# The first batch's input products of a selective scan on GpSimd instead of VectorE, with three state buffers

## The reference, cut to what matters

```python
def step(state, inp):
    d, b, c, u = inp
    dA = jnp.exp(d[..., None] * A)
    state = state * dA + (d * u)[..., None] * b[:, None, :]
    y = jnp.einsum('bdn,bn->bd', state, c)
    return (state, y)
```

## Time and profile before

| what | us |
|---|---|
| median of 3 runs | 1496.59 (1494.74 to 1496.68) |
| the profiled execution | 1496.58 |
| its span in the trace | 1494.8 |
| TensorE busy | 1345.9 (90% of the span) |
| VectorE busy | 1028.1 (69%) |
| ScalarE busy | 695.4 (47%) |
| GpSimd busy | 89.2 (6%) |

### The profile page before, as it was taken

How to read it: one execution, slowest core, us unless ns; L and a number is a source line. 1 busy time by engine, 2 the same in 40 slices (tenths; PEclk the granted TensorE clock), 3 DMA queues, 4 the chain that set the end, 5 groups by cost and what they waited for, 6 DMA issues and landing times.

```text
span 1494.8 us, 16001 instructions
## 1 busy us (share of the span) xinstructions
PE 1345.9 (90%) x5768; PEld 661.1 (44%) x5768; DVE 1028.1 (69%) x1219; ACT 695.4 (47%) x1477; POOL 89.2 (6%) x116
## 2 busy tenths in 40 slices
PE   5757668999999799899999799899999899799999
PEld 2324444444444365444444365444444355444443
DVE  5699996689979645789897844779897944521110
ACT  5345653465542285375552277365562187121110
POOL 0000001000000000000000000100000000100000
PEclk8955669999999799999999889999999999799999
DMA  6286661157765700137765610117775530012102
GB/s 232 46 197 145 136 146 29 53 138 189 189 148 126 176 2 1 43 106 181 180 162 141 164 45 2 39 53 189 190 166 144 144 83 2 0 33 63 59 25 85
DMA packets 53277, 158.80 MB, mean 106 GB/s; under 512 B 5072, under 2 KB 10704, under 8 KB 44752
## 3 DMA queue, kind: packets, MB, share of 16 engines
q0 software_dynamic: 9216, 67.11, 22.6%
q1 hardware_dynamic: 25664, 54.23, 11.1%
q10 hardware_dynamic: 18320, 36.45, 8.1%
HBM read 86.20 MB, written 4.46 MB: 61 GB/s over the span
## 4 chain that ended last, share of the span: by engine, by line
PE 68%; DVE 20%; ACT 6%; DMA 3%; issue 3%; ACTq 0%; POOL 0%; DVEq 0%
PE ps_a L854 21%; PE ps_a L866 10%; DVE state L1048 7%; PE ps_a L934 6%; PE ps_b L874 5%; PE ps_a L780 4%; PE ps_w L833 4%; PE ps_w L742 4%; PE ps_b L794 3%; DMA y_sb<-state 3%; DVE state L1053 3%; DVE state L1043 3%; ACT r L583 2%; DVE neg_max L1083 2%; PE ps_w L900 2%
## 5 line engine op out<-in xcount | busy, mean ns | idle before, releaser
L854 PE MATMUL ps_a<-xt,w_sb 128*128 128x512 f32 x704 | 319.2, 607 | 0.0
L1048 DVE TENSOR_TENSOR_SCAN state<-decay,state 128x2048 f32<-128x2048 f32 x64 | 282.7, 4418 | 2.1 <-DVE state L1043 0.5
L854 PEld LDWEIGHTS ps_a<-xt,w_sb 128*128 128x128 f32 x704 | 137.2, 196 | 173.2 <-issue 172.8
L635 ACT ACTIVATE r<-ps_a 128x512 f32<-128x512 f32 x132 | 78.8, 597 | 257.5 <-PE ps_a L866 137.5
L583 ACT ACTIVATE r<-ps_a,neg_max 128x128 f32<-128x128 f32 (+3 forms) x256 | 134.6, 542 | 131.8 <-DVE neg_max L1083 126.0
L1219 DVE TENSOR_TENSOR r<-r,ps_a 128x512 f32<-128x512 f32 x132 | 90.2, 685 | 149.9 <-ACT r L635 149.9
L934 PE MATMUL ps_a<-wd_sb,r 128*128 128x512 f32 x352 | 164.1, 617 | 17.0 <-DMA wd_sb<-in_w_down 16.8
L541 ACT ACTIVATE decay<-dt_sb,decay_rate 128x511 f32<-128x511 f32 x256 | 163.4, 711 | 30.1 <-DVE state L1048 29.7
L866 PE MATMUL ps_a<-r,wb_sb 128*128 128x512 f32 x352 | 166.6, 596 | 2.2 <-DVE r L1219 2.2
L780 PE MATMUL ps_a<-r 32*128 32x512 f32 (+3 forms) x512 | 125.7, 572 | 44.1 <-ACT r L583 40.0
L1043 DVE TENSOR_TENSOR state<-du_sb,bc_sb 128x2048 f32<-128x2048 f32 x64 | 146.2, 2284 | 7.8 <-DMA y_sb<-state 5.7
(11 more groups left out here) (117 smaller groups left out, 1385.3 us busy)
## 6 DMA issues: line engine op xcount, KB each, us to landing
y_sb<-state POOLq DMA_DIRECT2D x64, 1024.0 KB, 9.3
bc_sb<-bc_rows ACTq DMA_DIRECT2D x64, 512.0 KB, 6.1
w_sb<-in_w_tiles SPq DMA_DIRECT2D x44, 512.0 KB, 8.7
wd_sb<-in_w_down SPq DMA_DIRECT2D x44, 256.0 KB, 3.2
wb_sb<-in_w_adapt SPq DMA_DIRECT2D x44, 128.0 KB, 2.1
xa<-in_x SPq DMA_DIRECT2D x4, 1024.0 KB, 5.2
out_x<-xb SPq DMA_DIRECT2D x16, 256.0 KB, 8.0
xn_att<-in_ctx_t SPq DMA_DIRECT2D x4, 512.0 KB, 7.9
```

What stands on the lines that cost most here:

```text
L854: mm = nc.tensor.matmul(ps_a[:, 2 * (f % 2) + half, :], w_sb[:, slot, at + k * P:at + (k + 1) * P], xt[:, k, :], start=(k == 0), stop=Fals ...
L1048: nc.vector.tensor_tensor_scan(flat, decay[:, n % 2, :, :].rearrange("p j l -> p (j l)"), flat, 0.0, ALU.mult, ALU.add).then_inc(scan_chai ...
```

## The change

For batch 0 alone, the pieces `mul` of the states 1 to 15 leave VectorE; GpSimd does them as `spread` (state 0 stays on VectorE). GpSimd issues the add of `n` and then does `spread(n + 2)` (`spread(1)` comes first, as soon as `du_sb` is there). The state tiles and the row pairs of batch 0 go round three buffers instead of two: the third state tile lies in `r2`, the third pair of rows in the first half of `w_sb`'s first buffer. Therefore `spread(n)` waits for the add of `n - 3`, the load of row pair `n` for `out` of `n - 3`, and the first two loads of `w_sb` wait for the last `out` of batch 0. The table for batch 0 has 34 pieces instead of 49, again one in each of the eleven parts of the projections and the rest spread over 31 steps. The other batches keep their pieces, and only count their semaphores differently.

```diff
+FIRST_RING = 3
-def plan(counts):
+def plan(counts, first=False):
     pieces = [("du", 0)]
     for n in range(NS):
-        pieces += [("mul", n), ("run", n), ("out", n)]
+        pieces += [("mul", n)] * (n == 0 or not first) + [("run", n), ("out", n)]
...
-        slots[at["du", 0] if n < 2 else between(at["out", n - 2], at["mul", n])]["bc"].append(n)
+        ring = FIRST_RING if first else 2
+        used = at["mul", n] if ("mul", n) in at else at["run", n]
+        slots[at["du", 0] if n < ring else between(at["out", n - ring], used)]["bc"].append(n)
...
+PIECES_FIRST = 2 + 2 * NS
-PLAN_FIRST = plan([0] * DOWN + [1] * FT + spread_over(PIECES - FT, STEPS - LAST_STEPS) + [0] * LAST_STEPS)
+PLAN_FIRST = plan([0] * DOWN + [1] * FT + spread_over(PIECES_FIRST - FT, STEPS - LAST_STEPS) + [0] * LAST_STEPS, True)
...
+        states_first = [state[:, 0, :, :], state[:, 1, :, :], r2[:, 4:8, :]]
+        rows_first = [bc_sb[:, 0, :, :], bc_sb[:, 1, :, :], w_sb[:, 0, :].rearrange("p (c l) -> p c l", c=2)]
...
             def load_w(t, f):
                 if f >= 2:
                     sp.wait_ge(gu_ready, t * EVALS + EVAL_AT[f - 2, 0] + 1)
+                elif t == 0:
+                    sp.wait_ge(scan_chain, chain(0, NS - 1, 3))
                 else:
                     sp.wait_ge(scores_ready, t * STEPS + 1)
...
+            def spread(n):
+                if n == 1:
+                    pool.wait_ge(du_ready, 1)
+                if n >= FIRST_RING:
+                    pool.wait_ge(y_added, 16 * (n - FIRST_RING + 1))
+                slot, count = bc_use(0, n)
+                pool.wait_ge(bc_loaded[slot], 16 * count + 16)
+                row = rows_of(0, n)[:, 0, :].unsqueeze(1).to_broadcast([P, JT, L])
+                nc.gpsimd.tensor_tensor(state_of(0, n), du_sb[:], row, ALU.mult).then_inc(spread_ready, 1)
+
             def add_states(b, slot):
                 for n in slot["add"]:
...
+                    if b == 0 and n + 2 < NS:
+                        spread(n + 2)
...
             inverse_deviation("att", 0)
+            spread(1)
...
                 elif kind == "run":
...
-                    dve.wait_ge(scan_chain, base + 1)
+                    if b == 0 and n > 0:
+                        dve.wait_ge(spread_ready, n)
+                    else:
+                        dve.wait_ge(scan_chain, chain(b, n, 1))
```

More of the change, by code:

```diff
@@ L105, with chain, bc_use @@
 LAST_STEPS = 1
-PLAN_FIRST = plan([0] * DOWN + [1] * FT + spread_over(PIECES - FT, STEPS - LAST_STEPS) + [0] * LAST_STEPS)
+PLAN_FIRST = plan([0] * DOWN + [1] * FT + spread_over(PIECES_FIRST - FT, STEPS - LAST_STEPS) + [0] * LAST_STEPS, True)
 PLAN_NEXT = plan(IN_EVALS + spread_over(IN_DOWN, FT - FREE_DOWN) + [0] * FREE_DOWN +
                  spread_over(PIECES - sum(IN_EVALS) - IN_DOWN, STEPS - LAST_STEPS) + [0] * LAST_STEPS)
+def chain(b, n, k):
+    return 2 * n + k if b == 0 else PIECES_FIRST - 1 + (b - 1) * 3 * NS + 3 * n + k
+def bc_use(b, n):
+    if b == 0:
+        return n % FIRST_RING, n // FIRST_RING
+    slot = n % 2
+    return slot, (NS - slot + FIRST_RING - 1) // FIRST_RING + (b - 1) * (NS // 2) + n // 2
 def projections(f):
@@ L236, in decoder_layer, with state_of, rows_of @@
         xdt_sb = sb("xdt_sb", [P, L])
+        states_first = [state[:, 0, :, :], state[:, 1, :, :], r2[:, 4:8, :]]
+        rows_first = [bc_sb[:, 0, :, :], bc_sb[:, 1, :, :], w_sb[:, 0, :].rearrange("p (c l) -> p c l", c=2)]
+        def state_of(b, n):
+            return states_first[n % FIRST_RING] if b == 0 else state[:, n % 2, :, :]
+        def rows_of(b, n):
+            return rows_first[n % FIRST_RING] if b == 0 else bc_sb[:, n % 2, :, :]
         u_sb, xin_sb, conv_sb = state[:, 0, :, :], decay[:, 0, :, :], decay[:, 1, :, :]
@@ L305, in decoder_layer @@
         dt_ready = sem("dt_ready")
-        bc_loaded = [sem(f"bc_loaded{k}") for k in range(2)]
+        bc_loaded = [sem(f"bc_loaded{k}") for k in range(FIRST_RING)]
+        spread_ready = sem("spread_ready")
         decay_ready = sem("decay_ready")
@@ L461, in add_states @@
                     pool.dma_start(y_sb[:].rearrange("p j l -> p (j l)"),
-                                   state[:, n % 2, :, :].rearrange("p j l -> p (j l)"),
+                                   state_of(b, n).rearrange("p j l -> p (j l)"),
                                    accum_op=ALU.add).then_inc(y_added, 16)
+                    if b == 0 and n + 2 < NS:
+                        spread(n + 2)
             def attention(b, slots):
@@ L509, in split_first @@
                 if not first_batch(b):
-                    for k in range(2):
-                        act.wait_ge(bc_loaded[k], 16 * (NS // 2) * b)
+                    for n in range(NS - (FIRST_RING if b == 1 else 2), NS):
+                        slot, count = bc_use(b - 1, n)
+                        act.wait_ge(bc_loaded[slot], 16 * count + 16)
                 act.wait_ge(xdt_ready, b + 1)
@@ L523, in load_bc @@
                         act.wait_ge(bc_stored, 16 * b + 16)
[L524 to L527, removed]
+                    ring = FIRST_RING if b == 0 else 2
+                    if n >= ring:
+                        act.wait_ge(scan_chain, chain(b, n - ring, 3))
+                    elif b > 0:
+                        act.wait_ge(scan_chain, chain(b - 1, NS - 1, 3))
                     pair = bc_rows.rearrange("(c n) l -> n c l", c=2)[n]
-                    act.dma_start(bc_sb[:, n % 2, :, :], pair.unsqueeze(0).to_broadcast([P, 2, L]))\
-                        .then_inc(bc_loaded[n % 2], 16)
+                    act.dma_start(rows_of(b, n), pair.unsqueeze(0).to_broadcast([P, 2, L]))\
+                        .then_inc(bc_loaded[bc_use(b, n)[0]], 16)
             def make_decay(b, slot):
@@ L1032, in scan_piece @@
                     return
-                base = b * 3 * NS + 3 * n
-                flat = state[:, n % 2, :, :].rearrange("p j l -> p (j l)")
+                flat = state_of(b, n).rearrange("p j l -> p (j l)")
                 if kind == "mul":
@@ L1040, in scan_piece @@
                         dve.wait_ge(y_added, 16 * (b * NS + n - 1))
-                    dve.wait_ge(bc_loaded[n % 2], 16 * (NS // 2) * b + 16 * (n // 2) + 16)
-                    row = bc_sb[:, n % 2, 0, :].unsqueeze(1).to_broadcast([P, JT, L])
-                    tt(state[:, n % 2, :, :], du_sb[:], row, ALU.mult).then_inc(scan_chain, 1)
+                    slot, count = bc_use(b, n)
+                    dve.wait_ge(bc_loaded[slot], 16 * count + 16)
+                    row = rows_of(b, n)[:, 0, :].unsqueeze(1).to_broadcast([P, JT, L])
+                    tt(state_of(b, n), du_sb[:], row, ALU.mult).then_inc(scan_chain, 1)
                 elif kind == "run":
@@ L1050, in scan_piece @@
                 else:
-                    dve.wait_ge(scan_chain, base + 2)
-                    row = bc_sb[:, n % 2, 1, :].unsqueeze(1).to_broadcast([P, JT, L])
-                    tt(state[:, n % 2, :, :], state[:, n % 2, :, :], row, ALU.mult).then_inc(scan_chain, 1)
+                    dve.wait_ge(scan_chain, chain(b, n, 2))
+                    row = rows_of(b, n)[:, 1, :].unsqueeze(1).to_broadcast([P, JT, L])
+                    tt(state_of(b, n), state_of(b, n), row, ALU.mult).then_inc(scan_chain, 1)
             def rotate(b, f):
```

4 lines of the change are left out of this document (2 added, 2 removed).

## The result

The changed kernel takes 1529.79 us (median of four, 1526.06 to 1534.03) against 1496.61 (1494.74 to 1496.68): 1.0226 times as long, with an interval of 1.0193 to 1.0258. The direction was predicted and the size was not: 1509 was forecast, with 1525 as the upper end. The profiled execution took 1526.06 us with a span of 1524.1, 29.3 longer than before; in the other three the granted clock of TensorE was 0.902, 0.897 and 0.896 instead of 0.903, and the time longer with it. What follows explains the profiled 29.3; the 3.7 us by which the median lies above this execution were not traced.

What follows compares the result with a forecast made beforehand. VectorE was taken to bound batch 0's attention (busy 140.0 of 142 us), with adds close beneath at 10.1 us a state. +3.1 us in front and +9.3 in the attention gave +12.4, from 1496.58 to 1509 us; range 1482 to 1525.

Steps and rivals of the forecast that it cites:

- turns over SBUF for a whole instruction: `run` or `out` and `spread` exclude each other for whole instructions, first come first served; 1509 us, chance 0.75.
- the stretch in front: Ahead of batch 0's attention: `spread(1)` hidden, later products delay VectorE, `out(4)` ends at 109.5 instead of 106.44, +3.1 us.
- the edits at no cost: Late `w_sb` loads, covered by 39.8 us, row pairs loaded a state ahead and the last add's landing cost nothing.
- who goes first: In attention gaps of one step `run` precedes `spread`, 11.91 us a state, seven states; with two steps `spread` precedes, 13.17, three.
- second kind: Attention state with two steps ahead of `run`, so `spread` goes first: 1.26 + 4.42 + 4.32 + 0.98 + 2.19 = 13.17 us.
- the worst case of the turns: All ten attention states have `spread` first: 140.2 us, +18.1 and +3.1, total 1518.
- the terms of a state: Attention prices: `spread` 4.42 us, asking 1.26 behind `out`; step 0.98, `run` 4.32, `out` 2.19.
- The state behind them: Attention state after the ten, with no `spread` and two steps: 8.5 us.
- No exclusion: Rival: `spread` runs beside VectorE, adds 10.1 us apart, last `out` at 204.2, 24 us earlier, 1472 us; chance 0.13.
- Sharing: Rival: both engines go on, each slower; a state lies between 10.1 and 11.9 us, total 1493; chance 0.09.
- A quick GpSimd: Rival: `spread` takes VectorE's 2.27 us, taking turns; adds set 10.1 a state, total 1478 us; chance 0.03.
- L1138: Two-input VectorE instruction that kept its usual 0.69 us beside a small GpSimd product; cited as evidence against exclusion.

Runs made afterwards that it cites:

- one column: Changed kernel with each `spread` cut to 128x1, waits and order kept: median of ten 1475.08 us, ratio 0.9888.
- a fill that reads nothing: Changed kernel with each `spread` replaced by a GpSimd memset of the same 128x2048 tile to zeros: one run, 1464.75 us.
- layout alone: Changed kernel with all `mul` back on VectorE, three buffers and late `w_sb` loads kept: median of ten 1485.67 us, ratio 0.9974 to the kernel before.
- the quarters: Changed kernel with each `spread` cut into four instructions of 128x512: one run, 1537.46 us.
- The pause: Changed kernel with a 128x512 fill of another tile and a wait for it ahead of each `spread` but the first: one run, 1498.59 us.
- 4 and 512 columns: Changed kernel with each `spread` cut to 128x4 or 128x512 elements, operands still three-dimensional: 1473.80 us and 1486.64 us.
- the added wait: Changed kernel where `spread(n + 2)` also waits until `run(n + 1)` has ended: median of four 1510.15 us, ratio 1.0147 to the kernel before.

## Why the prediction was right, and where it failed

**Right: turns over SBUF for a whole instruction.** `run` or `out` beside a `spread` is lengthened by what is left of it and the other way round (88.36, 92.15, 109.95); one column behind a `run` waits 3.6 us, and a fill that reads nothing does not wait. The Trainium skill, SBUF — State Buffer, section Who interferes with whom, says that a VectorE instruction with two SBUF inputs contends with a GpSimd instruction that reads SBUF and not with one that only writes it. These runs agree on both halves: `run` at 9.44 beside the product, at 4.40 beside the fill. Maxima read PSUM and were left out of the turns; rightly, since one takes 0.42 at 141.18, inside a `spread` (138.04 to 142.85), as it did before (88.16).

**Right: the stretch in front.** `out(4)` ends at 109.36, forecast 109.5, and the times forecast from `run(1)` on are met within 0.4 each. `spread(1)` at 37.99 was hidden.

**Right: the edits at no cost.** With the layout alone the last add moves by 0.05 us. In the changed kernel the feed-forward part's first matmul, L902 now, starts 40.95 us behind `out(15)` (298.12 less 257.17); before it was 39.8. At most 1.1 us can be put to the late loads or to anything else there, and none of TensorE's waits between 255 and 330 us is for a load.

**Wrong: who goes first.** The step that failed is "With one step (0.98) in between, `run(n + 1)` is there first, `spread` follows it". VectorE did reach `run` first, in six of those seven states by 0.06 to 0.33 us (109.95 and 110.28, 150.50 and 150.78, 166.01 and 166.07, and three like them); in the seventh it came 0.94 late, held by ScalarE for 0.88 (125.28 and 124.34). In all seven `spread` went first. First come first served by the rows' starts does not hold for a large product directly behind an add: it wins where its row begins up to 0.33 us behind that of `run` (0.43 with the quarters, 101.83 and 101.40), and had lost at 0.66 (87.70 and 88.36) and 1.08 (98.49 and 99.57). The pause, which makes the distance 0.95 to 1.22, brings the predicted order back, and very nearly the predicted time. So all ten states are of the prediction's second kind: 131.7 instead of 122.9, **8.8 us** of what was missed. It stands in the prediction as the worst case of the turns, 1518, and would have been the better sum.

The rule was taken from small products: those at L451 stood still beside L988. With one column or four GpSimd loses such a tie, with 512 or 2048 it wins. The row was read rightly and carried over to a size for which it does not hold. The same page of the Trainium skill says that issue order and not the shape of the operation decides who blocks; by the rows' starts, size did decide here, at 0.28 us with 4 and 512 columns and at 0.06 with one and 2048 (166.70 and 166.76 with one column, 166.01 and 166.07 in the changed kernel). The quarters show a second thing that the prediction's turns leave out: with more queued, GpSimd keeps SBUF.

Size is not the whole of it, since in the run with the added wait (behind the run) the full product lost ties at 0.11 to 0.18. One count fits every tie of a large product in these runs: where it stands directly behind an add, its turn counts from the start of the add's issue. It won where `run` began 0.19 us or more behind that start (101.40 and 101.21 with the quarters; 0.29 or more in the changed kernel) and lost where `run` began ahead of it (87.70 and 87.75, 98.49 and 98.96). On that count GpSimd asks 0.30 to 0.43 us behind `out` and not the 1.26 of the prediction, ahead of a step of 0.98. This is a fit and not a test. The issue alone does not hold VectorE: with the pause `run` begins 0.35 behind it (146.35 and 146.00) and keeps its 4.40.

**Mis-sized: the terms of a state.** The ten states from `out(4)` to `out(14)` took 138.97 (109.36 to 248.33), 7.3 more than ten of the second kind at the prediction's prices. `spread` took 4.81 to 4.83 where 4.42 was taken: +4.0. Its row in a state begins 0.61 behind the add's and overlaps it by 0.28, and is 0.33 longer than alone (4.50). The Trainium skill, GPSIMD Engine Reference, section 3.1, has 4497 ns for an add of two inputs of 2048 float32 elements, which is the row at 37.99. The row of `spread` began earlier, 0.91 to 1.06 behind `out` instead of 1.26: −3.0. The steps between `run` and `out` took 15.5 us in the ten states, from 0.31 to 2.98, and not 0.98 each: +5.7. The sum took one step for each of the ten gaps, and four of them hold two (as from 159.90 to 162.88): fourteen steps, of 0.98 each, are 3.9 of the 5.7. Three of those four also hold a wait of 1.18 for ScalarE, as at 161.74. VectorE's list of waits between 88 and 259 us has

```profile
DVE r L1147 <- ACT r L650: 11.8, 6, 2.7
```

where it waited 0.6 us in all before. The other three of the six, 2.74 or 2.75 each, lie in the gaps of two steps from `out` to `run`, where `run` had to wait for `spread` in any case. Two small terms are left: `out` takes 2.27 to its end where the 2.19 to the next start was taken (+0.8), and `run` ends 4.29 behind `spread` and not 4.32 (−0.3). The five make the 7.3. The state behind them took 8.84, forecast 8.5.

**The sum.** Predicted +12.4, measured +29.3 of span: 8.8 for the turns, 7.3 for the terms, 0.3 for the last state, −0.1 in front, and 0.6 behind `out(15)`.

**The rivals.** No exclusion is out, but its time was right for work that does not hold VectorE up: it put the last `out` at 204.2, and the last add came at 205.90 with one column and 206.38 with the fill. Sharing is out: each instruction is whole. A quick GpSimd is out at 4.50.

**Open.** At which moment a large product takes SBUF, and at what size between 4 and 512 columns the tie turns: no size between them was run. With the added wait two things differ, no add directly ahead and `out` in the place of `run`, and no run separates them; in no kernel did a state's product stand ahead of the add. L1138, which kept its 0.69 beside a small product, is not explained by any run either.

## What to carry to other kernels

Before work moves from VectorE to GpSimd, ask of both sides whether they read SBUF: if so, the work isn't taken off VectorE but paid at GpSimd's price, here 4.8 us for 2.2, and of what was run here only a fill, which reads nothing, went beside it unhindered. Where two engines ask within some tenths of a microsecond of each other, cost both orders and forecast the dear one; and count the steps in each gap anew for the order that is costed. A short pause set the order at less cost here than a wait for the other engine's instruction (last add at 239.77 against 247.28). A third buffer was worth more for starting work in an idle stretch than for handing it to another engine.

## What had not been expected of the hardware

A row's start is no proof of a turn: a `run` that starts 0.06 to 0.33 us ahead of a large product directly behind an add can do nearly nothing until that product is through (up to 9.44 us for 4.40). Four products of 128x512 queued behind each other hold VectorE like one of four times the size (5.22 and 4.83). A fill of 128x2048 on GpSimd takes 1.80 us alone and 2.14 behind an add's issue, and lets VectorE go on.
